# A graph-network stack on one core: where the transposed adjacency comes from

## What is computed

```python
# layer 0: 8 attention heads, the adjacency is added to the weights
attn = softmax(q k^T) * .33 + .33 * adj + .33 * exp(-adj);  x = LN(x + attn v W_out + b)
# layer 1: hypergraph convolution, twice (512 hidden, then 256)
H = (adj != 0);  m = Be * (H^T xw);  out = Dn * (H m) + b
# layer 2: A_ij * exp(leaky_relu(s_j + s_i)), rows normalised, two products with it
# layer 3: agg = adj x / deg;  out = relu([x, agg] W^T)
```

## Time and profile before

| | |
|---|---|
| runs of the kernel before | 1293.24, 1293.99, 1295.88 us |
| profiled execution: its span | 1291.5 us (its own launch time isn't listed; what lies around the span is taken from the runs) |
| TensorE busy | 1247.2 us, 97% of the span |
| VectorE, ScalarE, GpSimd busy | 1068.8 (83%), 971.6 (75%), 478.5 us (37%) |
| DMA | 32.52 MB in 44293 packets, mean 25 GB/s |
| x: from issue to landing | 2.7 us (median of 32) |
| adjacency: from issue to landing | 2.1 us (median of 32) |

### The profile page before, as it was taken

How to read it: one execution, slowest core, us unless ns; L and a number is a source line. 1 busy time by engine, 2 the same in 40 slices (tenths; PEclk the granted TensorE clock), 3 DMA queues, 4 the chain that set the end, 5 groups by cost and what they waited for, 6 DMA issues and landing times.

```text
span 1291.5 us, 32910 instructions
## 1 busy us (share of the span) xinstructions
PE 1247.2 (97%) x9589; PEld 1110.3 (86%) x9589; DVE 1068.8 (83%) x3399; ACT 971.6 (75%) x2806; POOL 478.5 (37%) x1126
## 2 busy tenths in 40 slices
PE   6799999999999999999999999999999999999985
PEld 5688888888888888888898888898888898888874
DVE  3688888888888898888898888888888888888885
ACT  5477877777877777877777787778787777787773
POOL 3233444333443333443333343333343433344432
PEclk9899999999999999999999999999999999999998
DMA  6000100000000000000000100000001000000000
GB/s 214 17 8 21 26 25 25 16 16 18 25 25 25 22 11 17 25 25 25 25 9 17 25 25 25 25 8 19 23 25 25 25 8 23 20 25 25 17 9 9
DMA packets 44293, 32.52 MB, mean 25 GB/s; under 512 B 8176, under 2 KB 43120, under 8 KB 44272
## 3 DMA queue, kind: packets, MB, share of 16 engines
q1 hardware_dynamic: 42688, 31.47, 8.4%
q0 software_dynamic: 176, 0.52, 0.2%
q10 hardware_dynamic: 1408, 0.27, 0.1%
HBM read 23.87 MB, written 8.39 MB: 25 GB/s over the span
## 4 chain that ended last, share of the span: by engine, by line
PE 93%; DVE 3%; ACT 1%; issue 1%; DMA 1%; POOL 0%; DVEq 0%; SPq 0%; POOLq 0%; ACTq 0%
PE PS L405 15%; PE PS L406 15%; PE PS L409 15%; PE PS L494 5%; PE PS L548 5%; PE PS L495 5%; PE PS L498 5%; PE PS L528 4%; PE PS L538 4%; PE PS L584 3%; PE PS L568 2%; PE PS L598 2%; PE PS L520 2%; DVE ysb L1447 1%; PE PS L611 1%; PE PS L604 1%
## 5 line engine op out<-in xcount | busy, mean ns | idle before, releaser
L1722 POOL TENSOR_TENSOR rs<-mv,eps_c 128x1 f32<-128x1 f32 x256 | 61.2, 239 | 582.9 <-DVE mv L1208 581.4
L1726 POOL TENSOR_TENSOR rs<-rs,mhalf 128x1 f32<-128x1 f32 x320 | 176.3, 551 | 25.3
L891 ACT ACTIVATE prob<-PS,neg_max 128x128 f32<-128x128 f32 x512 | 179.7, 416 | 2.0 <-DVE neg_max L1272 2.0
L1285 DVE SCALAR_TENSOR_TENSOR prob<-prob,rl,gate 128x128 f32<-128x128 f32 x512 | 145.6, 347 | 1.5
L494 PE MATMUL PS<-xT_hi,wqk_hi 128*128 128x256 f32 x512 | 141.3, 297 | 0.0
L495 PE MATMUL PS<-xT_hi,wqk_lo 128*128 128x256 f32 x512 | 134.9, 285 | 0.0
L891 ACT ACTIVATION_READ_ACCUMULATOR prob<-PS,neg_max 128x1 f32 x512 | 131.4, 257 | 0.0
L1319 DVE SCALAR_TENSOR_TENSOR hid<-PS,Dn,b_bc 128x512 f32<-128x512 f32 x64 | 48.1, 751 | 85.4 <-PE PS L409 85.4
L498 PE MATMUL PS<-xT_lo,wqk_hi 128*128 128x256 f32 x512 | 103.5, 284 | 0.0
L494 PEld LDWEIGHTS PS<-xT_hi,wqk_hi 128*128 128x128 f32 x512 | 98.2, 192 | 5.3 <-issue 5.0
L495 PEld LDWEIGHTS PS<-xT_hi,wqk_lo 128*128 128x128 f32 x512 | 98.7, 193 | 0.0
(11 more groups left out here) (225 smaller groups left out, 4227.3 us busy)
## 6 DMA issues: line engine op xcount, KB each, us to landing
xin<-in_x_dram SPq DMA_DIRECT2D x32, 256.0 KB, 2.7
out_dram<-xout SPq DMA_DIRECT2D x32, 256.0 KB, 2.2
adj_in<-in_adj_dram SPq DMA_DIRECT2D x32, 128.0 KB, 2.1
wrow<-in_adj_dram SPq DMA_DIRECT2D x32, 128.0 KB, 4.5
wqkv_raw<-in_L_gnn_W_qkv_dram SPq DMA_DIRECT2D x1, 1536.0 KB, 7.6
w_raw<-in_L_gnn_W_dram SPq DMA_DIRECT2D x3, 512.0 KB, 11.4
mask_bc<-in_nodemask_dram SPq DMA_DIRECT2D x32, 32.0 KB, 2.8
wk_raw<-in_L_gnn_Wk_dram SPq DMA_DIRECT2D x3, 256.0 KB, 9.0
```

What stands on the lines that cost most here:

```text
L891: last = act.activation(prob[:, t, h, :], PS[:, bank, k * P:(k + 1) * P], ACT.Exp, bias=neg_max[:, t, h:h + 1], accum_out=row_sum[:, t, h: ...
L1285: last = dve.scalar_tensor_tensor(prob[:, t, h, :], prob[:, t, h, :], rl[:, t, h:h + 1], gate[:, t], ALU.mult, ALU.add)
L1726: return pool.tensor_tensor(rs[:, n, g, 1:2], rs[:, n, g, 0:1], mhalf[:], ALU.pow)
```

## The change

Only group 0 still has its adjacency transposed on TensorE. For all others, SyncE issues a DMA from HBM whose source is read transposed: `agT = adj.rearrange("g n m -> m g n")`. Partition m receives `adj[g, n, m]` for both graphs and all n. Neighbours in a partition lie 512 bytes apart in HBM, so each of the 32768 floats of a group is a run of its own, as in `beta_c`. In the loop this DMA is issued ahead of the one for x.

`adjT` is now written by a DMA, and its buffer must be free early. GpSimd therefore copies it to a new buffer `adjTc` right behind `fresid_`, and `carry` on ScalarE reads that one. The DMA for group i waits for `HT` and `adjTc` of group i - 1.

```diff
+        adjTc = at("adjTc", [P, G, P])
+        agT = adj.rearrange("g n m -> m g n")
+        def adjT_ready(eng, i):
+            if isinstance(i, int) and i == 0:
+                eng.wait_ge(act_adjT, 1)
+            else:
+                eng.wait_ge(t_in, i * 16)
...
-            def reload(i):
+            def load_x(i):
                 sp.wait_ge(pe_xT0, i)
                 sp.wait_ge(pool_resid0, i)
                 sp.sem_inc(sp_past, 1)
                 sp.dma_start(xin[:], xg[:, bass.ds(i * G, G), :]).then_inc(x_in, 16)
+            def load_adjT(i):
+                sp.wait_ge(dve_HT, i)
+                sp.wait_ge(pool_adjTc, i)
+                sp.sem_inc(sp_past, 1)
+                sp.dma_start(adjT[:], agT[:, bass.ds(i * G, G), :], allow_slow_non_contiguous=True).then_inc(t_in, 16)
...
-            reload(1)
+            load_x(1)
+            load_adjT(1)
+            load_mask(1)
+            load_adj(1)
             with sp.Fori(0, ITERS - 2) as j:
-                reload(j + 2)
+                load_adjT(j + 2)
+                load_x(j + 2)
+                load_mask(j + 2)
+                load_adj(j + 2)
                 store_group(j)
...
-                if L:
-                    after(pe, dve_o3, 2, s - 1, 1)
-                    adjT_(n)
                 if B:
                     T3_(j, 1)
...
             def carry(i):
                 act.wait_ge(pool_aT, i)
-                act.activation(adjTb[:], adjT[:], copy).then_inc(act_adjTb, 1)
+                act.wait_ge(pool_adjTc, i + 1)
+                act.activation(adjTb[:], adjTc[:], copy).then_inc(act_adjTb, 1)
...
-                if L:
-                    adjT_(n)
                 if B:
                     out_(j, 0)
...
-                    dve.wait_ge(act_adjT, i + 1)
+                    adjT_ready(dve, i)
                     dve.tensor_scalar(HT[:], adjT[:], 0.0, None, ALU.not_equal).then_inc(dve_HT, 1)
...
+                def adjTc_():
+                    adjT_ready(pool, i)
+                    pool.wait_ge(act_adjTb, i)
+                    settle(pool)
+                    pool.tensor_copy(adjTc[:], adjT[:]).then_inc(pool_adjTc, 1)
...
                     after(pool, act_x1, 2, s - 1, 2)
                     fresid_()
+                    adjTc_()
```

More of the change, by code:

```diff
@@ L234, in gnn_stack_kernel @@
         set_wjc = sem("set_wjc")
-        x_in, a_in, m_in, w_in, y_out = (sem(n) for n in ("x_in", "a_in", "m_in", "w_in", "y_out"))
+        x_in, a_in, t_in, m_in, w_in, y_out = (sem(n) for n in ("x_in", "a_in", "t_in", "m_in", "w_in", "y_out"))
         (pe_adjT, pe_xT0, pe_qk, pe_v, pe_AT, pe_S, pe_PT, pe_OT, pe_y0) = (
@@ L245, in gnn_stack_kernel @@
             sem("dve_" + n) for n in ("xT0", "HT", "mcol", "Be", "Dsum", "Dn", "max", "attn", "OT", "y0", "mv0", "deg"))
-        (pool_resid0, pool_gate, pool_rs0) = (sem("pool_" + n) for n in ("resid0", "gate", "rs0"))
+        (pool_resid0, pool_gate, pool_rs0, pool_adjTc) = (sem("pool_" + n) for n in ("resid0", "gate", "rs0", "adjTc"))
         (pe_ax, pe_h, pe_hT, pe_hw, pe_y1, pe_xT2, pe_Z01, pe_Z2, pe_si, pe_T1, pe_T2, pe_xT3, pe_Z3, pe_T3) = (
@@ L373, in reload, with load_mask @@
                 sp.dma_start(xin[:], xg[:, bass.ds(i * G, G), :]).then_inc(x_in, 16)
+            def load_adjT(i):
[3 more added lines that the diff above has]
+                sp.dma_start(adjT[:], agT[:, bass.ds(i * G, G), :], allow_slow_non_contiguous=True).then_inc(t_in, 16)
+            def load_mask(i):
                 sp.wait_ge(act_mbc, i * G)
@@ L378, in reload, with load_adj @@
                     .then_inc(m_in, 16)
+            def load_adj(i):
                 sp.wait_ge(dve_Dsum, i * G)
-                sp.wait_ge(pe_adjT, i)
+                sp.wait_ge(pe_adjT, 1)
                 sp.wait_ge(dve_deg, i)
@@ L471, in gate_sums, with adjT_first @@
                 last.then_inc(set_pe, 1)
-            def adjT_(i):
-                pe.wait_ge(a_in, i * 16 + 16)
+            def adjT_first():
+                pe.wait_ge(a_in, 16)
                 for g in range(G):
@@ L768, in first @@
                 w1_transposes()
-                adjT_(0)
+                adjT_first()
                 pe.wait_ge(set_copy, COPY_W2T)
@@ L801, in first @@
                 AT_(0)
-                adjT_(1)
                 pe.wait_ge(dve_y0, 2)
@@ L837, in high, with adjT_first @@
                         act.activation(hi, src, copy, scale=factor).then_inc(set_hi, 1)
-            def adjT_(i):
-                act.wait_ge(pe_adjT, i + 1)
-                act.wait_ge(act_adjTb, i)
+            def adjT_first():
+                act.wait_ge(pe_adjT, 1)
                 act.activation(adjT[:].rearrange("p g n -> p (g n)"), PS[:, bank_adjT, 0:G * P], copy).then_inc(act_adjT, 1)
@@ L1747, in gate_ @@
                     pool.tensor_tensor(flat, flat, mbc[:], ALU.mult).then_inc(pool_gate, 1)
+                def adjTc_():
[3 more added lines that the diff above has]
+                    pool.tensor_copy(adjTc[:], adjT[:]).then_inc(pool_adjTc, 1)
                 def rs0_(t):
                     scale_shift(step, NORM0, t, dve_mv0, i * G + t + 1, 2.0).then_inc(pool_rs0, 1)
-                return step, resid_, gate_, rs0_
+                return step, resid_, adjTc_, gate_, rs0_
             def back(j):
@@ L1783, in group @@
                 if F:
-                    fstep, fresid_, gate_, rs0_ = front(i)
+                    fstep, fresid_, adjTc_, gate_, rs0_ = front(i)
                 if B:
@@ L1814, in first @@
             def first():
-                fstep, fresid_, gate_, rs0_ = front(0)
+                fstep, fresid_, adjTc_, gate_, rs0_ = front(0)
                 pool.wait_ge(pool_const, 10)
```

## The result

The changed kernel takes 1670.46 us, the median of 4 runs (1668.33 to 1673.14), beside 1293.62 us for the kernel before: a ratio of 1.2914, 95% interval 1.2895 to 1.2933. That is 377 us more, where 507 were forecast. It lies inside the range, and the mechanism is the forecast's: x waits behind the element-wise DMA. What was too large is the length of that DMA; the cost of the clock was too small and made up for a part of it.

What follows compares the result with a forecast made beforehand. The prediction took TensorE to bound every stage; a 15.1 us stall for x plus 1.8 us of lowered clock, times 30, on 1291.5 gave 1798 us of span, 1801 us of time, with a range of 1580 to 3300 us.

Steps and rivals of the forecast that it cites:

- What bounds the kernel, and who waits: TensorE bounds each stage; x queues behind the new DMA and stalls TensorE 15.1 us in each of stages 1 to 30.
- The length of the DMA: The element-wise DMA of a group on SyncE's queue takes D = 24 us, 11.7 ns an element on each DMA engine.
- the lower end: Shortest DMA if nothing stands between elements: 9.1 ns each, 18.6 us, from the set-up's 4-byte packets; 1639 us in all.
- The slack: TensorE wants x at 385.4, so the stall is D - 8.9 us, D being the new DMA's time.
- GpSimd's copy: One added 128x256 copy on GpSimd, 0.74 us, hidden in 1.97 us of idle time: cost 0.
- The clock: After each gap TensorE runs at half its clock for 3.6 us of work, adding 1.8 us a stage.
- What goes at the stage's end: Two transposes and idle time on TensorE, at most 0.43 us a stage; gain 0 to 0.05, as `x1t` is due there.
- The sum: 1291.5 + 30 x (15.1 + 1.8) = 1798 us of span, 1801 us as measured time.
- Slower elements: Rival: elements of the new DMA take 20 to 37 ns; at 24.4 ns D is 50 us, total 2581 us; chance 0.22.
- elements served one at a time: Rival: all 16 DMA engines queue at the same rows, D = 374 us, time 12.3 ms; chance 0.06.
- Hidden: Rival: elements under 4.3 ns, or x overtaking on the queue, so nothing stalls; most likely 1293 us; chance 0.05.
- The rule that speaks against the change: Skill page: a DMA transposing by access pattern is 19 times slower than the DMA's own transpose; estimate 50 us, 2.6 ms total.

Runs made afterwards that it cites:

- Experiment 1: The changed kernel with the load of x issued ahead of the element-wise DMA in SyncE's loop: 1293.47 us beside 1293.31 for the kernel before, ratio 1.0002.
- experiment 5: The kernel before, nothing removed, with the same element-wise DMA added ahead of x into a buffer that nobody reads: 1666.61 us.
- experiment 3: The changed kernel with its new DMA loading only one block of the two, 16384 elements: 1304.74 us beside 1293.31 for the kernel before.
- experiment 4: The changed kernel with 80 transposes of the identity on TensorE ahead of those of x: 1594.8 us, ratio 1.2336 to the kernel before.
- experiment 2: The changed kernel with its new DMA reading the untransposed block in whole 512-byte rows: 1292.84 us beside 1293.31 for the kernel before, ratio 0.9999.
- experiment 6: The changed kernel with the loop's element-wise DMA issued by ScalarE on its own queue: 1293.52 us beside 1294.03 for the kernel before, ratio 0.9998.

## Why the prediction was right, and what in it was off

- **What bounds the kernel, and who waits.** Right: the stall sits on TensorE ahead of the transposes of x, once a stage, and microseconds there add in full. Experiment 1 shows it by taking x out from behind the DMA, experiment 5 by adding nothing but the DMA ahead of x, experiment 3 by its length.
- **The length of the DMA.** This term was mis-sized, and it is the largest part of the miss: 24 us forecast, 19.5 measured, 4.5 x 30 = 135 us. The working chose 11.7 ns an element, the slope by which issuing 256 and 512 runs occupies an engine's queue. Measured are 9.5 ns (9.4 by experiment 3), against 9.1 at the lower end, read from packets in flight. The row of the same kind of packet was the better basis; a slope through 256 more runs was stretched to 32768. That waits for HBM would add to 9.1 was argued; 0.4 came on top, and no run shows of what.
- **The slack.** 8.9 us forecast. With D = 19.5 and a stall of 9.8 it is 9.7, 0.8 x 30 = 24 us in all. The new DMA was to be issued 2.4 us behind the start of GpSimd's first instruction (371.40 to 373.8) and is issued 1.9 behind it (572.28 to 574.17): the copy takes 0.41 us, not 0.74 (next point), and from its end to the issue pass 0.24 us, not 0.4. The other 0.3 us are in the reading: the forecast took the start of a weight load, 385.4, for the moment at which TensorE wants x, and the idle time of 9.81 us is counted from the modelled end of the matmul ahead, 586.60.
- **GpSimd's copy.** Hidden, as forecast:

```profile
573.52 0.41 POOL L1775 COPY adjTc<-adjT 128x256 f32<-128x256 f32 x1
573.88 0.75 POOL L1788 TENSOR_TENSOR resid<-x1t,b_bc 128x256 f32<-128x256 f32 x1
576.24 0.73 POOL L1804 TENSOR_TENSOR aT_lo<-adjTb,aT_hi 128x256 fp32r<-128x256 f32 x1 [1.61 <-ACT aT_hi L956]
```

  The idle time ahead of L1804 shrank from 1.97 us to 1.61, by the copy.
- **The clock.** Right that it falls in each gap; 2.95 us a stage instead of 1.8, 35 us too little in all (21 by what experiment 4 gave back). The return was read from the set-up, where TensorE was partly busy before; after a gap of 9.8 us it took 5.9 us of work, not 3.6.
- **What goes at the stage's end.** Right that it is worth nothing (experiments 1 and 2), and that another wait takes its place. The one due first is `zb_lo`, VectorE's, 0.38 us, and the forecast didn't have it. `x1t`, which it named, is the next in line: L596's second half starts right behind it.
- **The sum.** The stall's mean over the 30 stages is (300.5 - 11.3) / 30 = 9.64 us, the 11.3 being the set-up's own. With the measured terms the same sum is 1291.5 + 30 x (9.64 + 2.95) = 1669 us of span; the profiled execution has 1668.0. That the forecast missed by only 130 us is in part luck: it had 164 us too much of stall and 35 too little of clock.
- **The rivals.** Slower elements and elements served one at a time fell with 9.5 ns. Hidden fell too, for elements on the path of x; that the same DMA is hidden once x stands ahead of it was not among the rivals and is the more useful half. x doesn't overtake on its queue.
- **The rule that speaks against the change.** The Trainium skill (VectorE: DVE Perf Modes, The three transpose paths) has the factor of 19 against the DMA's own transpose, for a large innermost stride at the destination. Here the stride is at the source and the elements are fp32, where its 1309 ns are for bf16, and no run has the DMA's own transpose; so the factor isn't tested. The estimate of 50 us that the forecast made of it doesn't agree with the trace, which has 21.0 us to landing. That such a DMA is slow does: whole rows land after 2.1 us in experiment 2. And with 21.5 us to landing the kernel of experiment 1 loses nothing, so the rule by itself doesn't decide.

## What to carry to other kernels

Price a transfer by its runs, and then ask what stands behind it on its queue and how much slack that has: here the order of two calls is worth 377 us and the transfer itself costs nothing. Take the price of a run from packets in flight rather than from the time that its issue occupies an engine. Taking work off the bounding engine pays only up to the next arrival that it waits for: 0.66 us a stage gave nothing in one order, 0.1 in another and all of it in a third, so look at what is due within a microsecond behind it.

## What was not expected of the hardware

- SyncE is held for 19.08 us at its next DMA instruction behind the 32768 runs, whichever that is (x after the change, the mask in experiment 1, 19.29 us). Behind half of the runs it is 9.68 us (experiment 3). ScalarE isn't held in experiment 6, where its next DMA comes a stage later; whether it would be at a DMA right behind was not tried.
- The DMA engines were busy 95% of the time from 586 to 595 us at 12 GB/s, and 94% from 590 to 594, where only elements moved, at 7 GB/s. In experiment 1, where the same traffic falls beside full work on all engines, no engine's work took longer (38.12, 32.70 and 29.65 us of TensorE, VectorE and ScalarE in a stage, against 38.27, 32.73 and 29.98).
- 4-byte elements leave 9.4 to 9.5 ns apart on each engine, with a fixed part of 1.8 us.
